# Two cross attentions of a twelve-layer kernel: key copies awaited pair by pair, steps dealt out anew, queries first, tables on GpSimd

## The reference, cut to what matters

```
q = norm(x) @ Wq        k = ctx @ Wk        v = ctx @ Wv        # ctx: 8 x 1601 x 256
second:  s = q k / 4, masked;            fourth: q, k divided by their norms, q times exp(min(scale, 4.6)), s = q k + fside (64 x 1601)
p = softmax(s);  x = x + (p v) @ Wo + b
```

## Time and profile before

| | us |
|---|---|
| median of 3 runs | 2891.72 (2889.15 to 2892.73) |
| the profiled execution | 2898.26, its span 2896.5 |
| l1x: opening, loop | 336 to 409, 409 to 797 |
| l3x: opening, loop | 2067 to 2153, 2153 to 2648 |
| PE, DVE, ACT, GpSimd busy, share of the span | 86%, 59%, 42%, 34% |

### The profile page before, as it was taken

One profiled execution on the slowest core, in us unless ns is written; L12 is line 12 of the kernel. 1 busy time (PEld: TensorE's weight loads), 2 busy tenths in 40 slices (PEclk: granted clock), 3 DMA queues, 4 the chain that ended last, 5 costly groups with the idle time before them and its releaser, 6 DMA issues. The chain is left out here.

```text
span 2896.5 us, 47169 instructions
## 1 busy us (share of the span) xinstructions
PE 2496.0 (86%) x18716; PEld 1609.7 (56%) x18716; DVE 1710.3 (59%) x3491; ACT 1224.8 (42%) x2195; POOL 972.9 (34%) x561
## 2 busy tenths in 40 slices
PE   8856879999978689999999998389868888898898
PEld 6733546666634356666666665145435555555655
DVE  6975255555485676767666652745564554553577
ACT  3342334444531244555545542344334454443344
POOL 6410213224042142244223400048633343434176
PEclk9976989999989889999999999799979999999999
DMA  4103332332120400100000000023322222220132
GB/s 114 50 1 110 97 89 69 104 81 63 35 95 3 133 28 28 29 1 28 29 28 4 1 1 7 23 72 104 104 57 62 71 58 62 70 57 19 35 93 68
DMA packets 86091, 158.19 MB, mean 55 GB/s; under 512 B 17401, under 2 KB 53970, under 8 KB 85874
## 3 DMA queue, kind: packets, MB, share of 16 engines
q1 hardware_dynamic: 82802, 146.79, 17.8%
q0 software_dynamic: 3072, 8.39, 1.0%
HBM read 115.16 MB, written 0.52 MB: 40 GB/s over the span
## 5 line engine op out<-in xcount | busy, mean ns | idle before, releaser
L3721 PE MATMUL PS<-l2x_rows,l2x_pth 128*128 128x512 f16 x832 | 281.5, 383 | 0.0
L3971 DVE TENSOR_TENSOR l2x_ptl<-PS,l2x_pth 128x512 f16<-128x512 f32 (+1 forms) x256 | 139.3, 586 | 207.0 <-ACT l2x_pth L3819 207.0
L98 PE MATMUL PS<-hot 128*128 128x512 f16 x452 | 135.1, 449 | 133.5 <-DVE l2a_t L2278 48.4
L3722 PE MATMUL PS<-l2x_rows,l2x_ptl 128*128 128x256 f16 x832 | 228.9, 275 | 0.0
L3564 POOL TENSOR_TENSOR l2x_rows<-l2x_rows,l2x_g 128x1024 f32<-128x1024 f32 (+1 forms) x28 | 58.7, 2096 | 404.8 <-DVE l2x_rows L3897 404.3
L3337 DVE CUSTOM_DVE_ANT_0 l1x_junk<-PS,l1x_bias 128x1024 bf16<-128x1024 f32 (+1 forms) x128 | 123.4, 992 | 111.4 <-PE PS L3005 110.6
L3205 ACT ACTIVATE l3x_pT<-PS 128x512 f32<-128x512 f32 (+1 forms) x208 | 122.1, 594 | 148.0 <-PE PS L3051 146.7
L3337 DVE CUSTOM_DVE_ANT_0 l3x_junk<-PS,l3x_bias 128x1024 bf16<-128x1024 f32 (+1 forms) x128 | 123.8, 992 | 83.1 <-PE PS L3005 82.5
L3819 ACT ACTIVATE l2x_pth<-PS 128x512 f16<-128x512 f32 (+1 forms) x256 | 117.9, 512 | 121.0 <-PE PS L3689 119.6
L98 PEld LDWEIGHTS PS<-hot 128*128 128x128 f16 x452 | 46.8, 111 | 209.0 <-DVE l2a_t L2278 49.2
L3652 PE MATMUL PS<-l2x_kh,l2x_qth 128*128 128x512 f16 (+1 forms) x512 | 129.3, 334 | 3.1 <-DVE l2x_shift L3917 1.6
(11 more groups left out here) (865 smaller groups left out, 6710.8 us busy)
## 6 DMA issues: line engine op xcount, KB each, us to landing
l2f_unit<-in_L_ffn_units_dram SPq DMA_DIRECT2D x36, 384.0 KB, 3.0
l3f_unit<-in_L_ffn_units_dram SPq DMA_DIRECT2D x34, 384.0 KB, 3.1
l1x_kst<-l1x_kh SPq DMA_DIRECT2D x128, 100.1 KB, 2.2
l3x_kst<-l3x_kh SPq DMA_DIRECT2D x128, 100.1 KB, 2.2
l2x_rows<-in_ctx_dram SPq DMA_DIRECT2D x8, 1536.0 KB
l1x_ctx<-in_ctx_t_dram SPq DMA_DIRECT2D x7, 1601.0 KB, 7.1
l3x_ctx<-in_ctx_t_dram SPq DMA_DIRECT2D x7, 1601.0 KB, 6.6
l1x_kst<-l1x_kl SPq DMA_DIRECT2D x64, 100.1 KB, 2.2
```

The lines of the kernel that those rows point to most:

```text
L98: self.nc.tensor.matmul(self.PS[:, bank, :], self.hot[:, 0:P], self.hot[:], start=True, stop=True)
L3721: nc.tensor.matmul(PS[:, ACC, :], pth[:, m, :], rows2[:, b % 2, m, :, :], start=(m == 0), stop=False)
L3722: last = nc.tensor.matmul(PS[:, ACC, 0:D], ptl[:, m, :], rows2[:, b % 2, m, 0, :], start=False, stop=(m == KT - 1))
L3971: v.tensor_tensor(ptl[:, m[0]:m[0] + len(m), :], PS[:, T_BANK + g % 2, 0:len(m) * P].rearrange("p (m n) -> p m n", n=P), pth[:, m[0]:m[0] ...
```

## The change

In both layers: the semaphore of the key copies is one for each pair of heads, and the copies go out pair by pair. The lists `steps` and `first` are dealt out anew. The queries' product Q stands first; in l3x DVE's work on them is in three items (Q, Z, Y) spread between the keys, in l1x in one (Y). GpSimd writes `one_hot` and `ident16` and adds b_o to X. After each A of the opening PE waits for both halves of `qst` and issues 3 or 2 warm-up products. `both` is a reduction over the two parts instead of a maximum of two slices. In l3x the table `bias_t`, its DMA and its scaling are gone.

```diff
     if normed:
-        steps = [[("K", 0, 0)], [("K", 0, 1)], [("N", 0, 0)], [("N", 0, 1), ("I", 0, 0)], [("V", 0, 0), ("U", 0, 0), ("I", 0, 1)],
-                 [("U", 0, 1), R_], [E], [("K", 1, 0)], [("K", 1, 1)],
-                 [O_, ("N", 1, 0)], [("N", 1, 1), ("I", 1, 0)], [A[0], ("U", 1, 0), ("I", 1, 1)],
-                 [P_, A[1], ("U", 1, 1)], [("V", 1, 0)], [A[2], A[3]], [("V", 2, 0)], [A[4], A[5]], [("V", 3, 0), A[6]], [A[7], A[8]],
-                 [A[9]], [("M", 0, 0), A[10]], [A[11]], [A[12], A[13]], [A[14]], [A[15]], [("M", 1, 0)]]
-        first = [("K", 0, 0), ("K", 0, 1), ("N", 0, 0), ("I", 0, 0), ("N", 0, 1), ("I", 0, 1), ("U", 0, 0), ("U", 0, 1), ("Q", 0, 0),
-                 ("K", 1, 0), ("K", 1, 1), ("F", 0, 0), ("N", 1, 0), ("N", 1, 1), ("I", 1, 0), ("I", 1, 1), ("T", 0, 0), ("U", 1, 0), ("U", 1, 1),
-                 ("V", 0, 0), ("V", 1, 0), ("T", 1, 0), ("V", 2, 0), ("V", 3, 0)] + A[:10] + [("M", 0, 0)] + A[10:] + [("M", 1, 0)]
+        steps = [[("K", 0, 0)], [("K", 0, 1)], [("N", 0, 0), R_], [("N", 0, 1), ("I", 0, 0)], [("U", 0, 0), ("I", 0, 1), ("V", 0, 0)],
+                 [E, ("U", 0, 1)], [("V", 1, 0)], [("K", 1, 0)], [("K", 1, 1)],
+                 [O_, ("N", 1, 0)], [("N", 1, 1), ("I", 1, 0)], [("U", 1, 0), ("I", 1, 1), ("V", 2, 0)],
+                 [P_, A[0], ("U", 1, 1)], [A[1], A[2]], [("V", 3, 0)], [A[3], A[4]], [A[5]], [A[6]], [A[7], A[8]],
+                 [A[9]], [("M", 0, 0), A[10]], [A[11]], [A[12]], [A[13], A[14]], [A[15]], [("M", 1, 0)]]
+        first = [("Q", 0, 0), ("K", 0, 0), ("K", 0, 1), ("N", 0, 0), ("N", 0, 1), ("I", 0, 0), ("Z", 0, 0), ("I", 0, 1), ("U", 0, 0),
+                 ("U", 0, 1), ("Y", 0, 0), ("V", 0, 0), ("V", 1, 0), ("K", 1, 0), ("K", 1, 1), ("N", 1, 0), ("N", 1, 1), ("I", 1, 0), ("I", 1, 1),
+                 ("T", 0, 0), ("F", 0, 0), ("U", 1, 0), ("U", 1, 1), ("T", 1, 0), ("V", 2, 0),
+                 ("V", 3, 0)] + A[:10] + [("M", 0, 0)] + A[10:] + [("M", 1, 0)]
     else:
-        steps = [[("K", 0, 0)], [], [("K", 0, 1)], [("K", 1, 0)], [R_], [("K", 1, 1)], [E], [("V", 0, 0)], [A[0]], [O_, A[1]],
+        steps = [[("K", 0, 0)], [], [("K", 0, 1), R_], [("K", 1, 0)], [E], [("K", 1, 1)], [("V", 0, 0)], [O_], [A[0]], [A[1]],
                  [("V", 1, 0), A[2]], [A[3]], [P_, A[4]], [("V", 2, 0), A[5]], [A[6]], [A[7]], [("V", 3, 0), A[8]], [A[9]],
                  [("M", 0, 0), A[10]], [A[11]], [A[12]], [A[13]], [A[14]], [A[15]], [], [("M", 1, 0)]]
-        first = [("K", 0, 0), ("K", 0, 1), ("Q", 0, 0), ("K", 1, 0), ("K", 1, 1), ("V", 0, 0), ("V", 1, 0), ("V", 2, 0),
-                 ("T", 0, 0), ("V", 3, 0), ("T", 1, 0)] + A[:10] + [("M", 0, 0)] + A[10:] + [("M", 1, 0)]
+        first = [("Q", 0, 0), ("K", 0, 0), ("K", 0, 1), ("K", 1, 0), ("K", 1, 1), ("Y", 0, 0), ("V", 0, 0), ("V", 1, 0),
+                 ("T", 0, 0), ("V", 2, 0), ("V", 3, 0), ("T", 1, 0)] + A[:10] + [("M", 0, 0)] + A[10:] + [("M", 1, 0)]
+    WARM = (3, 2)
...
-                    for g, part in enumerate((kh, kl, kh)):
-                        for j in range(RC):
+                    for j in range(RC):
+                        for g, part in enumerate((kh, kl, kh)):
                             sp.dma_start(kst[g * F:(g + 1) * F, b % 2, c * RC + j, :],
-                                         part[j * F:(j + 1) * F, c, :]).then_inc(stacked[c], 16)
+                                         part[j * F:(j + 1) * F, c, :]).then_inc(stacked[c * RC + j], 16)
...
+                for half in ((slice(0, S), slice(S, P)) if normed else (slice(0, P),)):
+                    of = k.ident[half, half if normed else slice(0, S)]
+                    link(nc.gpsimd.tensor_scalar(one_hot[half].rearrange("p (i s) -> p i s", s=S),
+                                                 of.unsqueeze(1).to_broadcast([of.shape[0], BANK // S, S]), ONE_HOT, None, ALU.mult))
+                nc.gpsimd.tensor_copy(ident16[:], k.ident[:]).then_inc(hot_made, 1)
...
+                st.wait(pool, "xn")
+                pool.wait_ge(loaded["rest"], 32)
+                nc.gpsimd.tensor_tensor(k.X[:], k.X[:], b_o[:].unsqueeze(1).to_broadcast([P, NT, D]), ALU.add).then_inc(x_ready, 1)
...
-                        if j == 0 and c % RC == 0:
-                            pe.wait_ge(stacked[c // RC], (b + 1) * STACK)
-                            if b == 0:
+                        if j == 0:
+                            pe.wait_ge(stacked[c], (b + 1) * STACK)
+                            if b == 0 and c % RC == 0:
...
                 for it in prepared:
                     item(it)
+                    if it[0][0] == "A":
+                        pe.wait_ge(q_act, 2)
+                        pe.wait_ge(q_dve, 2)
+                        k.warm(Q_BANK, WARM[it[0][2]])
...
-                        nc.scalar.activation(bias_t[:], bias_t[:], ACT.Copy, scale=S_SCALE)
...
-                            link(v.tensor_tensor(both[:, us], rmax[:, us, 0], rmax[:, us, 1], ALU.max))
+                            link(v.tensor_reduce(both[:, us], rmax[:, us, :], AX.X, ALU.max))
```

More of the change, by code:

```diff
@@ L2681, in context_attention @@
     assert len(steps) == STEPS
-    OFF_SLOT = "IUQTRF"
+    WARM = (3, 2)
+    OFF_SLOT = "IUQTRFZY"
     def at_step(b, s):
@@ L2711, in context_attention @@
     key_high, key_low, v_read = (k.sem(f"{name}_{s}") for s in ("key_high", "key_low", "v_read"))
-    stacked = [k.sem(f"{name}_stacked{c}") for c in range(NC)]
+    stacked = [k.sem(f"{name}_stacked{u}") for u in range(R)]
     constants, max_made, row_made = (k.sem(f"{name}_{s}") for s in ("constants", "max_made", "row_made"))
@@ L2775, in context_attention @@
             q = xn
-            qsq = n2[:, 0:NT * D]
-            q_high = n2[:, NT * D:NT * D + NT * D // 2].bitcast(F16).rearrange("p (t r f) -> p t r f", t=NT, r=R)
+            qsq = junk[:].rearrange("p a n -> p (a n)").bitcast(F32)
+            q_high = raw[:].bitcast(F16).rearrange("p (t r f) -> p t r f", t=NT, r=R)
             qn2 = sb("qn2", [P, NT * H])
@@ L2907, in split_keys @@
                             if h == 0 and b > 0:
-                                pool.wait_ge(stacked[c], b * STACK)
+                                for u in range(c * RC, (c + 1) * RC):
+                                    pool.wait_ge(stacked[u], b * STACK)
                             hold()
@@ L2945, in item @@
                     (kind, c, j), b = it
-                    if kind in "IURF":
+                    if kind in "IURFZY":
                         return
@@ L3108, in item @@
                     (kind, c, j), b = it
-                    if kind == "Q":
+                    if kind == "Z":
                         if normed:
@@ L3112, in item @@
                             q_scales.end(nc.scalar.activation(qn2[:], qn2[:], ACT.Ln), "ln")
+                    elif kind == "Y":
+                        if normed:
                             q_scales.wait(act, "exp_in")
@@ L3140, in item @@
                             if j == 0 and b > 0:
-                                act.wait_ge(stacked[c], b * STACK)
+                                for u in range(c * RC, (c + 1) * RC):
+                                    act.wait_ge(stacked[u], b * STACK)
                             nc.scalar.activation(kh[:, c, at:at + n], slot_banks(it)[:, 0:n], ACT.Copy,
@@ L3253, in item @@
                             link(v.tensor_scalar(q_scale[:], q_scale[:], MAX_SCALE, None, ALU.min))
+                    elif kind == "Z":
+                        if normed:
                             q_scales.wait(dve, "ln")
@@ L3257, in item @@
                                 q_scale[:].unsqueeze(1).to_broadcast([P, NT, H]), ALU.mult, ALU.add), "exp_in")
+                    elif kind == "Y":
+                        if normed:
                             q_scales.wait(dve, "exp")
+                            qf = q[:].rearrange("p t d -> p (t d)")
+                            heads = lambda a: a.rearrange("p (n d) -> p n d", d=DH)
                             link(v.tensor_tensor(heads(qf), heads(qf), qn2[:].unsqueeze(2).to_broadcast([P, NT * H, DH]),
@@ L3264, in item @@
                             link(v.tensor_scalar(alive[:], alive[:], 1.0, None, ALU.min))
+                            st.wait(dve, "q")
+                            qv = PS[:, Q_BANK:Q_BANK + 2, :].rearrange("p b n -> p (b n)")
                             for t in range(NT):
@@ L3270, in item @@
                         st.end(last, "q_three")
-                        for i in range(BANK // S):
-                            if normed:
-                                v.tensor_scalar(one_hot[0:S, i * S:(i + 1) * S], k.ident[0:S, 0:S], ONE_HOT, None, ALU.mult)
-                                last = v.tensor_scalar(one_hot[S:P, i * S:(i + 1) * S], k.ident[S:P, S:P], ONE_HOT, None, ALU.mult)
-                            else:
-                                last = v.tensor_scalar(one_hot[:, i * S:(i + 1) * S], k.ident[:, 0:S], ONE_HOT, None, ALU.mult)
```

(4 more changed lines are left out.)

18 lines of the change are left out of this document (8 added, 10 removed).

## The result

The changed kernel takes 2844.25 us, median of 4 runs (2838.89 to 2852.0); the kernel before, on the same chip, 2891.35 (2889.15 to 2892.73). Ratio 0.984, 95% interval 0.9813 to 0.9867. Forecast 2838, range 2820 to 2866. The profiled execution took 2840.62, its span 2839.1.

What follows compares the result with a forecast made beforehand. PE was taken as first in line in both loops, with waits and a low clock in the openings. Gains 8.3 + 5.3 + 13.0 + 29.1 − 2.0 = 53.7 us bring the profiled 2898.3 to 2844.6, median 2838; range 2820 to 2866.

Steps and rivals of the forecast that it cites:

- likeliest case: Whole kernel: the forecast's own case, a time within 2828 to 2848 us, chance 0.52.
- 1: Rival, l3x's loop: waits come back at the banks, 6.2 a cycle instead of 4.0, +15 us, 2853; chance 0.20.
- 3: Rival, both openings: warm-ups run at the low clock, 9 us more per stage and 6 us gained lost, 2862; chance 0.06.
- l1x's opening, 8.3: Second cross attention's opening: earlier first maximum 7.2, second K's low clock -1.7, maxima 3.4 and -1.5, loop start 0.9.
- l1x's loop, 5.3: Second cross attention's loop: V0's wait 6.8 and O's 2.0 go, the second group's K costs 3.5.
- l3x's opening, 13.0: Fourth cross attention's opening: first maximum 8.0 us earlier, run of maxima 2.5 shorter, loop start at full clock 2.5.
- l3x's loop, 29.1: Fourth cross attention's loop: PE's waits of 57.1 us fall to 4.0 in each of 7 cycles.
- Moved work, -2.0: Both stages: tables and X+b_o moved to GpSimd can hold up DVE; 2.0 us charged, bounds 0 and 8.1.
- 2: Rival, l3x's loop: key copies land as late as before, A8 waits 6.0 a cycle, +42 us, 2880; chance 0.08.
- 4: Rival, l3x: DVE's stall at M0 is really gone, 7 × 1.0 + 2.3 us, 2829; chance 0.06.
- 5: Rival, l3x's loop: GpSimd delivers the next context late, making the kernel slower, up to 2915; chance 0.04.
- 6: Rival, both stages: nothing gained, each wait replaced by its like, the openings by the context, about 2891; chance 0.04.

Runs made afterwards that it cites:

- run 4: The changed kernel without the five warm-up matmuls per pair of the opening's maxima and without the wait for both query copies: 2874.39 us.
- second profile: The changed kernel measured again with no edit: 2861.77 us, ratio 0.9866 to the kernel before.
- Run 5: The changed kernel with maxima taken as scaled minima and one reduction writing the 16-bit row, without the separate scaling: 2829.57 us, ratio 0.9749.
- run 3: The changed kernel with key copies issued part by part for each group of four pairs, as before: 2908.79 us, ratio 1.0019 to the kernel before.
- run 7: The changed kernel with three of ACT's four mask sums moved behind the copies of the first keys in l1x's opening: 2859.8 us.
- run 9: The changed kernel with `both` as a two-operand maximum again, the scaling behind it kept: 2848.08 us.

## Why the prediction was right, and where its steps were off

The direction, the likeliest case and the range held; the forecast was 6 us low by the medians. Its sum was 53.7 against 43.2 in the two stages, so it was 10.5 too high where it was made. That the median lies in the likeliest case (2828 to 2848) has luck in it: 2891.35 less the 43.2 is 2848.2, and the few us below that come from stages that I hadn't priced. Of the signs that I named, one didn't come: the first maxima are 4.0 us earlier in both stages, and not 7 to 8. One came by half: the clock in the run of maxima is 1.00 in l1x, but 0.85 in l3x. The others came. Two bounds of the range were added up wrongly: its lower terms reach 2817 and not 2820, and rivals 1 and 3 together give 2877 and not 2866.

- **l1x's opening, 8.3:** measured 7.0 to the loop's start, where 7.4 of it lay. PE stood idle 6.71 us ahead of the second K and ran some 3 us long behind it, where I took 1.7. The clock in the run of maxima was 1.00, so the 1.5 charged for it didn't come; run 4 prices the warm-ups. The new order of the openings itself had no run of its own.
- **l1x's loop, 5.3:** with the 0.9 of its start 6.2, measured 4.3. Over the whole stretch behind the opening the wait of V (6.8) and that of A behind O (2.0) are gone, as forecast; M waits 1.5 and A on a key copy 0.4 less. But the second K waits 8.5 for DVE's ticks, 8.2 more than before, where I had 3.5. The view of waits also lists 5.1 us of new ones at the turned scores (L3062), in 32 pieces of up to 0.2. I don't count them: of the 144 mask products that stand ahead of these (L3059) the trace has 105, and all 144 of their weight loads, so that these are most likely gaps in the record. Without them the waits fall by 2.5, and 1.9 comes from the first ten us of the loop, with the clock at 1.00 and not 0.81: 4.4 for the measured 4.3.
- **l3x's opening, 13.0:** the term that was most off: 10.5 of it lay ahead of the loop, and measured are 5.3 (3.6 in the second profile); the other 2.5 came as about 2.1, the first ten us of the loop having the clock at 1.00 for 0.79. Two steps of it. The first gives the 4.0 by which the first maximum missed. I gave DVE's second query part 5.2 us, alone; it now runs beside GpSimd's split of the first keys and takes 10.0 (2078.66 to 2088.68):

```profile
2080.71 2.99 POOL L2920 TENSOR_TENSOR l3x_kl<-l3x_k,l3x_kh 128x1024 f16<-128x1024 f32 x1
...
2081.75 2.50 DVE L3249 TENSOR_SCALAR l3x_raw<-l3x_xn 128x1024 f16<-128x1024 f32 x1
...
2089.95 4.98 PE L2995 MATMUL PS<-l3x_sq,l3x_ones 128*128 128x512 f32 x8 [5.96 <-DVE l3x_k L3319]
```

  The same L3249 takes 0.69 us in l1x, where GpSimd is idle. I listed such overlap only for the moved tables, not for the moved queries. But not all of it came through: counted from the stage's start, DVE began this part at 26.5 and not at 28.5, so the last `k32` was done at 38.4 for my 36.9, 1.5 late. N, which I had end at 38.3, ended at 42.7, 4.4 late: PE stood idle 5.96 us ahead of it, and its eight products took 4.98 us, where the first N's took 3.01. The kernel before had shown that, 5.81 behind 14.56 of idle time, and I had priced N at the full clock. From N to the first maximum the delay stays at 4.0 to 4.4. No run moved the queries out of the overlap, so what it is worth alone stays open. The second step: `minus` stalled 2.16 us in the run of maxima and the clock stood at 0.85 there. Run 5 takes 18.2 us for that run and not 22.2: 4.0, where 2.3 was charged.
- **l3x's loop, 29.1:** measured 26.6 with those 2.1, so 24.5. Copies, R and E came as forecast; in an undisturbed cycle the waits are 2.4, under my 4.0. Three cycles have a wait of 5.2 to 6.6 at M: the step of the sum that was mis-sized, 1.5 a cycle around M0. Up to the last M PE's waits sum to 34.5 where 28 was forecast. Over the whole stretch PE's idle time falls by 22.3 (60.3 to 37.9) and its busy time by 4.3 (433.95 to 429.68), of which 2.1 is the clock at the loop's start and 2.2 no term of mine had.
- **Moved work, -2.0:** run 8, with the tables back on DVE, moves l3x's first maximum by 3.6 to 5.2 us, but its stages are not told apart from scatter. So neither that the move pays nor the 2.0 that I charged is shown.
- **Rivals.** 1 (residue 6.2 a cycle): measured 4.9, between it and my case, but by three stalls, not by late maxima. 2: run 3 makes it, 41 to 43 for my 42, though by another sum: A8 waits 4.8 a cycle and not 6.0, and the clock and M do the rest. 3: the clock stayed up in l1x (1.00) and mostly in l3x (0.85); in run 7 it came true for 6 us, with 3.46 a pair for my 3.5. 4 was priced at 9.3; with the stall really gone it is 27.5 to 29.3 in l3x and 3.8 in l1x, where no stall over 0.74 us was: M's waits, 1.9 in its loop, go altogether, and the rest isn't explained. That is the largest mis-sizing: I had priced one us a cycle, and not three long stalls with their low clock. 5 and 6 didn't occur.

## What to carry to other kernels

A four-element instruction can be the dearest of a loop: look at the longest duration of a group, not its median, and compare its end with GpSimd's. Price a wait of PE with the slow stretch behind it (7.8 us for 5.2 here), and two edits of one chain together, since one alone may lose (+12.4) what both win (-26.6). When work is moved to another place, ask what else runs there. Before a small difference between two profiles is read, look how much the same stage moves where it wasn't edited (548.9 to 553.5 here).

## What the runs showed of the hardware

- DVE's `tensor_scalar` waited for the GpSimd instruction that ran when it started: 4 elements per row took 5.77 us for 0.17, ending 0.02 behind it, and 1024 took 2.50 for 0.69. The two-operand maximum did the same (2.77 for 0.16 before, up to 5.95 in run 9). Reductions of the same data never did (0.160 to 0.163 in 16), those that write 16 bits neither (run 5).
- Behind a wait of 5.17 us PE had the clock at 0.50 for 2.9 us, and at 0.63 in the next 4.
- The same gap of 2.47 us on PE was followed by a clock of 1.00 in one kernel and of 0.54 in another.
- A stage that no edit touches took 87.9, 90.4 or 97.8 us; between 90.5 and 97.8 the windows show the granted clock to differ (0.86 and 0.50 at the same place).
